# Attention denominators on Trainium2: sums over four key steps, joined by accumulating transfers

## The reference

```python
h = _sln(hidden, w, ln_g, ln_b, Wg, bg, Wb, bb)
qkv = (h @ Wqkv.T + bqkv).reshape(B, N, num_heads, hd, 3)
q, k, v = (moveaxis(qkv[..., i], 2, 1) for i in range(3))   # in short
energy = jnp.einsum('bhqd,bhkd->bhqk', q, k)
att = jax.nn.softmax(energy, axis=-1) / D ** 0.5
out = jnp.einsum('bhqk,bhkd->bhqd', att, v)
...
out = out @ Wp.T + bp
h1 = out + hidden
h2 = _sln(h1, w, ln_g, ln_b, Wg, bg, Wb, bb)
return h2 + h1
```

## Time and profile before

| | |
|---|---|
| median of three runs | 1943.48 us (1940.95 to 1946.12) |
| the profiled execution | 1942.7 us, of which the profile's span is 1940.7 us |
| attention | from about 930 us to about 1825 us of the span |
| TensorE, DVE, ACT, POOL busy | 96%, 65%, 40%, 59% of the span |
| granted TensorE clock, mean | 0.984 of full speed |

### The profile page before, as it was taken

How to read it: one execution, slowest core, us unless ns; L and a number is a source line. 1 busy time by engine, 2 the same in 40 slices (tenths; PEclk the granted TensorE clock), 3 DMA queues, 4 the chain that set the end, 5 groups by cost and what they waited for, 6 DMA issues and landing times. The chain is left out here.

```text
span 1940.7 us, 28963 instructions
## 1 busy us (share of the span) xinstructions
PE 1868.3 (96%) x10616; PEld 1260.3 (65%) x10616; DVE 1256.3 (65%) x2056; ACT 775.2 (40%) x1376; POOL 1145.6 (59%) x588
## 2 busy tenths in 40 slices
PE   6699999999999899999999999999999999999996
PEld 1578888888887788888555555555555555555584
DVE  4546555555656454547677777777777777777299
ACT  1332122123122222221466666666666666666300
POOL 1565664465464212111577877787778777877555
PEclk9899999999999999999899999999999999999998
DMA  7301011110103555473743334433433344312494
GB/s 243 130 1 55 22 36 51 48 38 22 54 1 120 186 177 195 162 238 129 170 100 91 87 88 111 110 92 86 108 92 84 93 110 101 91 48 88 174 394 155
DMA packets 117692, 212.51 MB, mean 110 GB/s; under 512 B 18598, under 2 KB 36134, under 8 KB 117576
## 3 DMA queue, kind: packets, MB, share of 16 engines
q1 hardware_dynamic: 93980, 190.60, 33.0%
q10 hardware_dynamic: 23408, 20.37, 3.4%
q0 software_dynamic: 192, 0.05, 0.0%
HBM read 134.40 MB, written 75.80 MB: 108 GB/s over the span
## 5 line engine op out<-in xcount | busy, mean ns | idle before, releaser
L1459 DVE TENSOR_REDUCE at_mrow<-banks 128x1 f32<-128x512 f32 x984 | 600.6, 683 | 189.6 <-PE banks L1308 189.5
L1556 POOL TENSOR_TENSOR at_pair<-at_probs 128x2048 f32<-128x2048 f32 x127 | 581.7, 4580 | 185.5 <-ACT at_probs L1439 185.3
L1439 ACT ACTIVATE at_probs<-banks 128x512 f32<-128x512 f32 x1024 | 516.1, 624 | 258.9 <-PE banks L1324 258.9
L1324 PE MATMUL banks<-early_qs,early_ks 98*128 98x512 f32 x1024 | 410.1, 419 | 1.9 <-ACT at_probs L1439 1.8
L1308 PE MATMUL banks<-early_ks,early_qs 96*128 96x512 f32 x984 | 406.3, 413 | 3.7 <-DMA at_v<-v_scratch 1.9
L1324 PEld LDWEIGHTS banks<-early_qs,early_ks 98*128 98x128 f32 x1024 | 193.9, 190 | 114.1 <-ACT at_probs L1439 94.5
L1308 PEld LDWEIGHTS banks<-early_ks,early_qs 96*128 96x128 f32 x984 | 186.6, 190 | 109.5 <-issue 63.1
L1336 PE MATMUL banks<-at_probs,at_v 128*32 128x512 f32 x2048 | 253.6, 601 | 0.0
L71 PE MATMUL banks<-l_ht,l_weights 128*128 128x512 f32 x768 | 179.3, 393 | 5.8 <-ACT l_gt L595 5.8
L71 PE MATMUL banks<-qk_nt,l_weights 128*128 128x512 f32 x768 | 179.8, 392 | 3.0 <-ACT qk_gt L949 3.0
L71 PE MATMUL banks<-l_weights,l_hf 128*128 128x512 f32 x768 | 177.2, 390 | 0.0
(11 more groups left out here) (127 smaller groups left out, 2101.6 us busy)
## 6 DMA issues: line engine op xcount, KB each, us to landing
qk_scratch<-qk_out SPq DMA_DIRECT2D x64, 512.0 KB, 2.8
early_ks<-qk_scratch SPq DMA_DIRECT2D x48, 512.0 KB, 7.1
early_qs<-qk_scratch SPq DMA_DIRECT2D x96, 256.0 KB, 4.4
attn_scratch<-at_out SPq DMA_DIRECT2D x32, 512.0 KB, 4.4
o_a<-attn_scratch SPq DMA_DIRECT2D x32, 512.0 KB, 13.8
v_scratch<-qk_v ACTq DMA_DIRECT2D x32, 256.0 KB, 2.4
at_v<-v_scratch SPq DMA_DIRECT2D x16, 512.0 KB, 3.5
o_x<-x_scratch SPq DMA_DIRECT2D x8, 1024.0 KB, 16.1
```

The source lines that it names most:

```text
L1324: pe.matmul(et[n % 3][:], ks[0:98, slot, j, (i % KC) * P:(i % KC + 1) * P], qs[0:98, slot, i // KC, j, :], start=True, stop=True).then_inc ...
L1439: nc.scalar.activation(probs[:, i % 4, j, :], et[n % 3][:], ACT.Exp).then_inc(exp_done, 1)
L1459: nc.vector.tensor_reduce(mrow[:, half, keys, u:u + 1], em[n % 3][:], AX.X, ALU.max).then_inc(max_done, 1)
L1556: nc.gpsimd.tensor_tensor(psum2[:, pair % 2], probs[:, a], probs[:, a + 1], ALU.add).then_inc(pair_ready, 1)
```

## The change

- **Sums of four steps.** POOL still makes one addition per pair. The sum of an even pair goes into one of two buffers of `sums`, that of an odd pair into a third; behind it POOL issues a transfer from SBUF to SBUF of the whole 128 x 2048 tile (1 MB) that adds the third buffer onto the first (`accum_op=ALU.add`, semaphore `quad_ready`). `den` runs once for such a quad, after `av` of the odd pair that comes two pairs later (`LAG = 3`). The next odd pair's addition waits for the transfer, since it reuses the third buffer. At the very end `den` takes three tiles directly rather than two.
- **Turns.** `LEAD` becomes 6: the M products of the next group begin at pair 2, 48 of them are made in the projection stage, and `turn_max` stands at pairs 2 and 6 ahead of `av`, in the denominators' bank; it waits for `den_taken`, and the first `den` of a half waits for `negt_taken`.
- **Loads in three parts.** SP loads the stack of group g+2 in three parts (two key transfers; one key transfer and three of queries; three of queries and the values), each behind a wait for a quad's transfer to land. For the last group the same places load the operands of the output projection. The stack of group 1 is loaded at the end of the projection stage.
- **Order within a group.** On SP `place_neg` now stands ahead of `widen_rden`, and behind `store`; ACT copies the denominators after steps 3 and 11 rather than 1 and 9, and DVE inverts them at pairs 2 and 6 rather than 1 and 5. On POOL `multiply`, `round_off`, `remain` stand at pairs 0, 1, 2 and 4, 5, 6; the product goes in place into `av_sb`, and `round_off` is a copy of it rather than a second multiplication.

```diff
@@ load_stack_keys, load_stack_queries: take the rows to load @@
@@ qkv_stage, SP, behind the last step @@
+            sp.wait_ge(qk_done, NM * NCH)
+            load_stack_keys(sp, sh, sh.early_ks, 1, 0)
             sp.wait_ge(sh.negt_taken, 1)
             ...
+            for half in range(QH):
+                load_stack_queries(sp, sh, sh.early_qs, 1, 0, half)
@@ attention_stage @@
-        TURN = (SWITCH + PAIRS // 2 - 1, SWITCH - 1)
+        TURN = (SWITCH + PAIRS // 2, SWITCH)
+        QUADS = PAIRS // 2
+        LAG = 3
@@ SP @@
+            def load_part(g, slot, part):
+                if QUADS * (g - 2) + part > 0:
+                    sp.wait_ge(quad_ready, 16 * (QUADS * (g - 2) + part))
+                if part == 0:
+                    if g > 2:
+                        sp.wait_ge(av_done, STEPS * (g - 2))
+                    load_stack_keys(sp, sh, ks, g, slot, (0, 1))
+                if part == 1:
+                    load_stack_keys(sp, sh, ks, g, slot, (2,))
+                    load_stack_queries(sp, sh, qs, g, slot, 0)
+                if part == 2:
+                    load_stack_queries(sp, sh, qs, g, slot, 1)
+                    load_v(g, slot)
             def group(g, slot, nth=None, first=False, load=True, with_next=True):
+                fetch(0)
                 if not first:
                     spread_den(g - 1, 1)
+                    store(g - 1, 0)
+                place_neg(g, slot, 1)
+                if not first:
                     widen_rden(g - 1, 1)
+                fetch(1)
+                fetch(2)
                 spread_den(g, 0)
                 if not first:
                     store(g - 1, 1)
                 if with_next:
                     place_neg(g + 1, (slot + 1) % RING, 0)
+                widen_rden(g, 0)
@@ PE @@
-            def den(g, pair):
-                pe.wait_ge(pair_ready, PAIRS * g + pair + 1)
+            def den(g, quad):
+                q = QUADS * g + quad
+                pe.wait_ge(quad_ready, 16 * (q + 1))
+                ...
+                    pe.wait_ge(negt_taken, min(halves(g, quad * QH // QUADS) + 1, QH * G))
             def den_before(g, p):
-                if p > 0:
-                    den(g, p - 1)
+                if p >= LAG:
+                    den(g, (p - LAG) // 2)
                 elif g > 0:
-                    den(g - 1, PAIRS - 1)
+                    den(g - 1, QUADS + (p - LAG) // 2)
+                    if p == TURN[1]:
+                        turn_max(g, 1)
+                    if with_next and p == TURN[0]:
+                        turn_max(g + 1, 0)
                     av(g, slot, 2 * p)
+                    av(g, slot, 2 * p + 1)
+                    if p % 2 == 1:
                         den_before(g, p)
@@ POOL, for each pair @@
+                    quad, second = divmod(PAIRS * g + pair, 2)
                     pool.wait_ge(exp_done, HG * (STEPS * g + 2 * pair + 2))
+                    if second and quad >= 1:
+                        pool.wait_ge(quad_ready, 16 * quad)
+                    if not second and quad >= 2:
+                        pool.wait_ge(den_done, quad - 1)
+                    into, a = sums[:, 2 if second else quad % 2], 2 * pair % 4
+                    nc.gpsimd.tensor_tensor(into, probs[:, a], probs[:, a + 1], ALU.add).then_inc(pair_ready, 1)
+                    if second:
+                        pool.wait_ge(pair_ready, PAIRS * g + pair + 1)
+                        pool.dma_start(sums[:, quad % 2].rearrange("p j c -> p (j c)"), into.rearrange("p j c -> p (j c)"),
+                                       accum_op=ALU.add).then_inc(quad_ready, 16)
```

More of the change, by code:

```diff
@@ L922, in step @@
                         if last and t < TT - 1:
-                            for n in islice(maxima, 1):
+                            for n in islice(maxima, 1 + k % 2):
                                 maximum(s, n)
@@ L1035, in step @@
                     if loads is None and t < TT - 1:
-                        for n in islice(maxima, 4):
+                        for n in islice(maxima, 6):
                             take_maximum(n)
@@ L1195, in _, with load_projection @@
         def _(sp):
-            def load_keys(g, slot):
-                load_stack_keys(sp, sh, ks, g, slot)
-            def load_queries(g, slot, half):
-                load_stack_queries(sp, sh, qs, g, slot, half)
+            def load_part(g, slot, part):
[11 more added lines that the diff above has]
+                    load_v(g, slot)
+            def load_projection(g, part):
+                sp.wait_ge(quad_ready, 16 * (QUADS * g + part))
+                if part == 0:
+                    sp.wait_ge(av_done, STEPS * g)
+                    for half in range(QH):
+                        sp.wait_ge(out_free[half], 16 * (KT + 1))
+                    load_attended(sp, sh, 0)
+                if part == 1:
+                    load_residual(sp, sh, 0)
+                    for b in range(2):
+                        load_style(sp, sh, b)
+                if part == 2:
+                    load_attended(sp, sh, 1)
+                    load_residual(sp, sh, 1)
             def load_group(g, slot):
@@ L1313, in turn_max @@
                 pe.wait_ge(max_done, 2 * UNITS * halves(g, half))
+                if halves(g, half) > 2:
+                    pe.wait_ge(den_taken, halves(g, half) - 2)
                 for keys in range(2):
-                    last = pe.matmul(turn_bank(g, half)[0:UNITS, keys * P:(keys + 1) * P], mrow[:, half, keys],
-                                     sh.ident[:], start=True, stop=True)
+                    last = pe.transpose(den_ps[0:UNITS, keys * P:(keys + 1) * P], mrow[:, half, keys], sh.ident[:])
                 last.then_inc(mrow_turned, 1)
@@ L1398, in _ @@
             groups(pe, group)
-            for n in (2, 3):
+            pe.wait_ge(pair_ready, PAIRS * G - 1)
+            tiles = [sums[:, (QUADS * G - 1) % 2], probs[:, 2], probs[:, 3]]
+            for tile in tiles:
                 for j in range(HG):
-                    last = pe.matmul(den_ps[HD * j:HD * (j + 1), :], ones_col[:], probs[:, n, j, :], start=False, stop=n == 3)
+                    last = pe.matmul(den_ps[HD * j:HD * (j + 1), :], ones_col[:], tile[:, j, :], start=False, stop=tile is tiles[-1])
             last.then_inc(den_done, 1)
@@ L1423, in take_den @@
             def take_den(g, half):
-                act.wait_ge(den_done, KC // 2 * halves(g, half))
+                act.wait_ge(den_done, QUADS // QH * halves(g, half))
                 if not (isinstance(g, int) and g == 0):
@@ L1443, in group @@
                         take_av(g, i // KC)
-                    if i == 1 and not first:
+                    if i == 3 and not first:
                         take_den(g - 1, 1)
-                    if i == KC + 1:
+                    if i == KC + 3:
                         take_den(g, 0)
@@ L1494, in group @@
                         negate_max(g + 1, 0)
-                    if p == 1 and not first:
+                    if p == 2 and not first:
                         invert(g - 1, 1)
-                    if p == SPAN + 1:
+                    if p == SPAN + 2:
                         invert(g, 0)
```

115 lines of the change are left out of this document (36 added, 79 removed).

## The result

The changed kernel takes **1960.67 us** (median of four runs, 1958.12 to 1964.36), beside 1944.11 for the kernel before on the same chip: a ratio of 1.0088 with a 95% interval of 1.0066 to 1.0110, so it is 0.9% slower. The forecast was 1895.

A forecast was written before the change was run, and what follows sets the result against it. TensorE, busy all of a group's 55.54 us, bounds the kernel, with ACT close behind. 1942.7 - 55.7 + 1.0 + 3.0 + 2.1 - 3.7 + 5 = 1894.4, with 0.8 for the median 1895.2, called 1895; range 1876 to 1915.

The forecast's parts named there:

- traffic: DMA engines in attention: transfers kept apart from loads, not stores; 0.3 us a group, +5 in all (0 to 25).
- den: TensorE in the attention loop: half of the `den` runs go, 64 x 0.87 = -55.7 us (-67 to -45).
- the rival that ACT takes back half of the gain: Shorter attention pairs wait for an earlier exponential's bank, each `den` worth 0.45: +27, about 1922; chance 0.05.
- Turns: 31 turns on TensorE in attention, now delaying the first `av` by about the same 0.41: 0 us (-12 to +6).
- POOL: POOL's queue in attention: copies at most 1.29 us, issues 1.1; 48.8 of a group's 52.1 us, not the bound.
- POOL's rival: POOL's issues at 2.2 us each need 53.2 us a group instead of 52.1: +18, about 1913; chance 0.07.
- The transfer alone: 1 MB accumulating transfer: lands 6.6 us after its issue ends, 7.7 with issue; 8.4 affordable, break-even 9.3.
- the loop through the third buffer: POOL's addition, issue, landing, next odd addition: 4.58 + issue + landing within two pairs' 13.0 us, leaving 8.4.
- The start: Group 0 of attention: loading group 1's stack ahead removes ACT's wait of 5.49 before pair 3: -3.7 us.
- The end: Both ends of attention: more M products in the last projection chunk 1.9, last group's pair saves 0.29: +2.1 us together.
- The negatives: Negatives queued on SP behind the store, a microsecond missing twice a group: +32, about 1927; chance 0.09.
- The rival on the slower side: Accumulating transfer's issue plus landing over 9.3 us lengthens all 62 loops: +50, about 1993; chance 0.24.

The follow-up runs named there:

- small_acc: Changed kernel with loads whole, but the accumulating transfer adds only 16 of 2048 columns (8 KB): 1884.92 us, ratio 0.9687.
- experiment 1: Changed kernel, but from group 3 on the second load part (1.25 MB) moves only one row per transfer: 1897.77 us, ratio 0.9760.
- experiment 7: Changed kernel with the second load part issued ahead of `widen_rden` on SP: 1989.67 us, ratio 1.0227.
- Experiment 11: `four_parts` with group 1's queries issued behind group 0's values at the start of attention: 1909.46 us, ratio 0.9820.
- experiment 9: `four_parts` with the negatives issued ahead of the stores: 1901.11 us, ratio 0.9776.
- experiment 8: Changed kernel with the negatives placed ahead of the 512 KB store in both halves: 1953.48 us, ratio 1.0042.
- four_bal: Changed kernel with loads in four parts of 1.25, 0.5, 1.25 and 0.5 MB: 1909.11 us, ratio 0.9816.
- four_parts: Changed kernel with loads in four parts of 1.0, 0.5, 1.25 and 0.75 MB, the last behind `widen_rden`: 1910.55 us, ratio 0.9819.
- two_parts: Changed kernel with loads in two parts, all keys (1.5 MB), then queries and values (2 MB): 1974.29 us, ratio 1.0143.
- experiment 4: The same run as `small_acc`: changed kernel with the accumulating transfer cut to 16 columns (8 KB), loads whole: 1884.92 us, ratio 0.9687.

## Why the prediction was wrong

The forecast failed by its sign, and mainly by one term, the one for traffic. Point by point:

- **`den`, right.** 5.97 and 6.84 came as written. ACT lags by nothing worth naming, and the rival that ACT takes back half of the gain falls.
- **Turns, a little better.** Undisturbed, a pair with a turn takes 6.20 (1229.37 to 1235.57), so a turn costs 0.23 and not 0.41 ahead of `av`. `take_den` costs nothing where I gave it 3 us. Both together make a group 51.75 where I had 52.1, and `small_acc` 1884.9, 5 us under the 1890 that my sum gives without traffic.
- **POOL, about right.** An issue takes 0.87 (I said 1.1), and `round_off` as a copy 0.82 in the mean, 0.60 with nothing merged beside it, against the 1.29 that I allowed. POOL's rival falls.
- **The transfer alone, right.** 6.9 to 7.2 from the start of the issue, undisturbed; I expected 7.7, could afford 8.4, and put the break-even at 9.3. The Trainium skill, "Collectives: The Full Stack", section "The bandwidth ceiling: the fold count and why AG ≠ RS ≠ AR", has a reduction at half the copy's rate. By that rule, with the start-up of 2.0 us that the same skill gives in "DMA: Bandwidth & Descriptors", section "Anatomy of one DMA — SWDGE (gpsimd) path", 1 MB takes 6.8, an estimate; the trace agrees, with 6.9 to 7.2. The plain rate would have made it 4.4; the trace doesn't.
- **Which wait a late transfer ends, only named.** I priced the loop through the third buffer. The wait that holds the pair is the other one, TensorE's read of the quad: in the changed kernel `den` of quad 1 is due 8.2 to 9.1 us after the start of the issue (1244.67 to 1253.58 in the rows above), and the quad that lands in 11.7 stops TensorE for 2.5 to 3.6 us; the pair of the rows is longer by 9.76 - 6.84 = 2.9. POOL's wait in the loop is longer (4.44), and its next transfer starts late by it, yet in ten of twelve groups that one still lands ahead of its own `den` (in the others TensorE waits 0.4 and 0.6). So the 3.3 that my loop gives (11.7 - 8.4) comes near by luck. The loop also has 0.30 between the addition and the issue that I left out. The halves with pairs 0 to 3, whose quads land in 7.5 and 8.2 in the mean, stay at 26.1.
- **Traffic, wrong.** I took 0.3 us a group, +5 in all, at most 25. The share of the DMA engines came near what I worked out (0.72, against 42 of 52 or 0.81), but I read a share of busy time where what counts is who runs beside whom. The step that failed is the sentence that the transfers "are kept apart from the loads by waits". I had the order on SP before me, with `widen_rden` ahead of the second part, and did not follow it: SP gets past it some 3.7 us after the landing, and 1.25 MB then start with the next transfer. From `small_acc` to the changed kernel are 76 us. 63 of them go with part 1 (experiment 1), and the same bytes issued on the landing bring quad 1 from 11.7 to 8.5 (experiment 7).
- **Of the loss a third is the clock.** TensorE idles 42 of 820 us in attention. At 56.9 us a group rather than 51.75 the stretch loses 820 x 5.1 / 56.9 = 74. The other 30 or so are mostly slower work: the granted clock is 0.97, since 48 of the 820 us stand at half speed, and so 24 us of full-speed work are missing. I had no term for it. Some 8 us stay open. Two stretches of the changed kernel show it, a long wait and what follows:

```profile
1306.00:1312.00 6.00, 3.33 (x22) 1.10 (x21) 2.70 (x5) 2.17 (x5) 1.58 (x2) 1.00 0.78 162
1312.00:1316.00 4.00, 3.86 (x23) 2.70 (x24) 1.78 (x3) 1.78 (x3) 3.77 (x1) 0.66 0.60 152
1316.00:1322.00 6.00, 6.00 (x28) 3.41 (x27) 4.72 (x10) 3.47 (x6) 4.44 (x4) 0.66 1.06 247
1322.00:1328.00 6.00, 6.00 (x36) 3.20 (x36) 4.95 (x9) 4.03 (x8) 3.93 (x2) 1.00 0.56 154
```

  With TensorE idle for 2.7 of 6 us, the clock goes down for part of the next 10 (a mix of 1.2 and 2.4 GHz; the products of the front start 0.43 us apart there, 0.24 at full clock) and then back. It doesn't follow on every wait: behind the one at 1254 the clock stays at 1.00.
- **The start, wrong.** The 5.49 of the earlier trace rows is gone, but one of 5.51 stands in pair 1, and the first exponential is at 934.49 rather than 931.34. By the first copy of `av` both kernels are even (962.68 and 962.56), so the term is 0 and not -3.7. Experiment 11 shows why: SP has group 1's queries and two groups' values to fetch there, 2.5 MB, and the one that is last is waited for.
- **The end.** From the last copy of `av` to the end are 121.2 us rather than 118.0, +3.1 against a forecast of +2.1 for both ends of the stage. The larger loss comes before that copy: in the last group the projection's operands stand beside the transfers, which land in 13.1 and 12.5, with a wait of 5.71 on TensorE, and the half takes 7.7 us more than before. In `small_acc` it takes 1.7 more. My sum had no term for it, and the best kernel still has it (quad 1 of the last group lands in 11.8 in experiment 9).
- **The negatives, half right.** That rival had its place right: the median landing went from 1.8 to 5.1, behind the store. Its size was 7 to 9 us (experiments 8 and 9), not 32. Ahead of the store they still take 4.0 (experiment 8), so it isn't mainly the store that holds them.
- **The rival on the slower side** had the direction right, and its cause wrong. It wanted a transfer that is slow by itself, in each of 62 loops (+50); what came is one in four at 11.7. That was the missing case: one quad a group, late for TensorE.

## What to carry to other kernels

A wait that keeps two transfers apart only says when the later one may start at the earliest; read what stands ahead of it in its queue, and when that lets it go. Where a loop has a spare of a microsecond, work out each of its turns with the bytes that are in flight beside it, since one in four that collides cost here more than all that was gained. And cut loads so that little of a piece is left in flight when the next critical transfer begins; measure when its last load lands, not its bytes. Here 3.5 MB in four pieces of 0.5 to 1.25 MB made a loss of 0.9% into a gain of 1.8%, and 2.2% with the small urgent copies ahead of the large store.

## What the runs showed of the hardware that I had not expected

- An accumulating transfer from SBUF to SBUF of 128 x 2048 float32 (1 MB) takes 0.87 us of POOL to issue and 6.9 to 7.2 to land, 8 KB of it 2.0; the difference is 5 us, or some 210 GB/s. The issue takes 0.87 us for the 8 KB too, which also lie in 128 rows; 8 KB in four rows took 0.56.
- How late it lands goes with when the last load beside it lands. Counted from the start of its issue, means over twelve groups: load at 1.6 us, transfer at 7.6 (`four_bal`, quad 3); 2.4, 7.8 (`four_parts`, quad 0); 3.6, 8.9 (`four_bal`, quad 0); 3.7, 8.2 (`four_parts`, quad 1, only 0.5 MB); 4.5, 9.2 (`four_parts`, quad 3); 5.8, 11.3 (`two_parts`, quad 2); 7.8, 11.7 (changed kernel, quad 1, 1.25 MB issued 1.5 us ahead, 10.9 to 12.2). Beside 0.5 MB it was 6.9 to 8.8 in one kernel (`four_bal`) and 7.0 to 9.7 in another (`four_parts`).
- The copies of 8 KB for the negatives take 1.8 us in the kernel before, and 5.1 behind a store of 512 KB beside an accumulating transfer. With the small transfer of experiment 4 they are back at 1.8, behind the same store; ahead of the store, beside the 1 MB, they take 4.0 (experiment 8) and 4.8 (experiment 9). So it is the accumulating transfer that holds them, and the store adds a little.
- The two products of a turn cost 0.23 us ahead of `av` and 0.41 behind it. Why wasn't tested.
